# Ternary weights decided on VectorE beside an attention stage, in another order, and a token mixer's row-maximum scores one place ahead

## The reference

```python
# layer 0: token mixer (q, k, v are 32 rows each), attention, feed-forward with ternary weights
h = tok(x)                                   # softmax(q'k / sqrt(32)) v over 512 tokens, 128 sequences
h = h + attn0(layernorm(h))                  # 32 query heads, 8 key heads, head size 16, rope
h = h + ffn0(layernorm(h), w1, w3, w2)
# layer 1: attention, then a feed-forward with 4-bit weights
def ternary_quant(w):                        # of w1, w3 (1365 x 512) and w2 (512 x 1365)
    s = jnp.mean(jnp.abs(w))
    return jnp.clip(jnp.round(w / s), -1.0, 1.0) * s
```

## Time and profile before

| | us |
|---|---|
| median of 3 runs | 2435.5 |
| lowest and highest of the 3 | 2434.01, 2435.65 |
| the profiled execution's own time | 2430.69 |
| its span in the profile | 2428.5 |
| mean granted TensorE clock of it | 0.978 |
| PE busy in the span | 2243.3 (92%) |
| DVE busy | 1666.4 (69%) |
| ACT busy | 1495.8 (62%) |
| POOL busy | 1008.6 (42%) |

### The profile page before, as it was taken

The page is one execution under the profiler, slowest core; times in us unless marked ns, Lnnn a source line. Parts: engine busy times, 40 slices in busy tenths (PEclk is TensorE's granted clock), DMA queues, the critical chain, the costliest instruction groups (busy, mean ns, idle before and its releaser), DMA issues. The chain is left out here.

```text
span 2428.5 us, 41174 instructions
## 1 busy us (share of the span) xinstructions
PE 2243.3 (92%) x13188; PEld 1128.8 (46%) x13188; DVE 1666.4 (69%) x2937; ACT 1495.8 (62%) x2398; POOL 1008.6 (42%) x1002
## 2 busy tenths in 40 slices
PE   7999999998999994999999994999986999999998
PEld 2333333335666662444444443666652344444443
DVE  6666666656889886555556734666647888888874
ACT  4666666667787793445455514676645666667673
POOL 1222222238777771022223402444434555555552
PEclk9999999999999997999999997999998999999999
DMA  5544544532343211122222212222211111111101
GB/s 147 138 126 131 136 129 127 149 88 66 117 139 94 66 54 49 48 76 76 73 77 88 66 57 91 81 85 82 78 53 41 31 44 49 40 53 44 44 27 52
DMA packets 144444, 195.00 MB, mean 80 GB/s; under 512 B 32789, under 2 KB 76405, under 8 KB 144298
## 3 DMA queue, kind: packets, MB, share of 16 engines
q1 hardware_dynamic: 116890, 157.48, 21.5%
q10 hardware_dynamic: 27408, 35.66, 5.3%
HBM read 125.17 MB, written 42.21 MB: 69 GB/s over the span
## 5 line engine op out<-in xcount | busy, mean ns | idle before, releaser
L339 DVE TENSOR_REDUCE tm_negmax<-tm_s 128x1 f32<-128x512 f32 x512 | 323.3, 679 | 164.3 <-PE tm_s L382 164.0
L301 ACT ACTIVATE tm_prob<-tm_s 128x1024 f32<-128x1024 f32 x256 | 257.6, 1023 | 136.5 <-PE tm_s L402 130.7
L2271 PE MATMUL f_part<-f_xhi,gu 128*128 128x512 f16 x704 | 269.1, 382 | 18.3 <-ACT f_firstg L2090 6.6
L2271 PE MATMUL f_part<-f_xlo,gu 128*128 128x512 f16 x704 | 268.3, 381 | 0.0
L419 PE MATMUL tm_o<-tm_prob,tm_vt 128*64 128x512 f32 x1024 | 255.7, 620 | 0.0
L2059 POOL TENSOR_TENSOR f_firstg<-f_firstg,f_secondg 128x512 f32<-128x512 f32 x88 | 150.6, 1711 | 190.6 <-DVE f_secondg L2167 190.6
L2293 PE MATMUL f_pz<-dn,f_ghi 128*128 128x512 f16 x704 | 214.1, 379 | 5.8 <-ACT f_zc L2122 5.8
L382 PE MATMUL tm_s<-tm_qk 96*128 96x512 f16 x512 | 199.1, 391 | 14.8 <-DMA tm_qk<-tm_xs 14.3
L262 POOL TENSOR_TENSOR tm_hn<-tm_nd,tm_rows 128x1024 f32<-128x1024 f32 x32 | 75.3, 2353 | 292.9 <-DMA tm_rows<-rden 292.9
L402 PE MATMUL tm_s<-tm_qk 98*128 98x512 f16 x512 | 194.0, 382 | 1.3 <-DMA tm_qk<-tm_mrow 1.3
L969 PE MATMUL a_bankB<-a_wo,a_yThi 128*128 128x512 f16 x512 | 156.3, 388 | 4.1 <-DVE a_yTlo L892 4.0
(11 more groups left out here) (193 smaller groups left out, 5658.6 us busy)
## 6 DMA issues: line engine op xcount, KB each, us to landing
tm_qk<-tm_xs SPq DMA_DIRECT2D x384, 64.0 KB, 2.1
tm_xqk<-in_qk ACTq DMA_DIRECT2D x32, 512.0 KB, 4.4
a_hin<-h SPq DMA_DIRECT2D x64, 256.0 KB, 2.7
a_hres<-h SPq DMA_DIRECT2D x64, 256.0 KB, 3.0
h<-a_hout SPq DMA_DIRECT2D x64, 256.0 KB, 2.5
f_hin<-h SPq DMA_DIRECT2D x64, 256.0 KB, 2.8
f_hres<-h SPq DMA_DIRECT2D x64, 256.0 KB, 2.8
tm_vt<-in_vt ACTq DMA_DIRECT2D x32, 256.0 KB, 3.0
```

What stands on the lines that cost most here:

```text
L301: nc.scalar.activation(prob[b][:, 2 * h:2 * h + 2, :], s2[:, i % 2, :, :], ACT.Exp, scale=SCALE).then_inc(exp_done, 1)
L339: nc.vector.tensor_reduce(negmax[u][:, m:m + 1], s1[:, p % BANKS, :], AX.X, ALU.max, negate=True).then_inc(s1_read, 1)
L2271: last = nc.tensor.matmul(part[q % BANKS][:, :], (gate, up)[which][:, j, m * P:(m + 1) * P], xparts[x][u][:, j, :], start=x == 0, stop=x == 1)
```

## The change

It does five things.

1. `LEAD` becomes 15: the maximum scores run one place further ahead, and the numbers of the bank uses shift with it.
2. The down matrix is loaded first (n = 5 to 8) and the gate and up blocks after it (n = 9 to 16). VectorE sums the down blocks at n = 7 to 12, ScalarE the others at n = 11 to 18.
3. There are two totals: one of the down matrix at n = 14 and one of gate and up at n = 20, each with its own wait of TensorE for VectorE.
4. VectorE decides the down blocks one by one at the ends of steps 15 to 20, not after steps 32 and 33.
5. ScalarE's Sign and Relu are gone. VectorE decides a gate or up block with an is_lt (now L1329) and the `scalar_tensor_tensor` (now L1331), at the ends of steps 22 to 29.

```diff
-    LEAD = 14
+    LEAD = 15
@@ place, turned, use, freed @@
-        return 0 if m == 0 else m + 1 if m < 9 else m + 2
+        return m if m < 2 else m + 1 if m < 10 else m + 2
-        return 1 if pair else 10
+        return 2 if pair else 11
-            return p - (p > 1)
+            return p - (p > 2)
-            return 0 if t == 0 and p - BANKS == 1 else use(t, p - BANKS) + 1
+            return 0 if t == 0 and p - BANKS == 2 else use(t, p - BANKS) + 1
@@ ternary_weights @@
-    def totals(pe, tiles):
-        pe.wait_ge(summed, 8)
+    def totals_down(pe, tiles):
         pe.wait_ge(summed2, last // 2 + 1)
         pe.wait_ge(att.q_copied, tiles)
-        nc.tensor.matmul(total, ones[:, :], rows[:, :, :].rearrange("p i c -> p (i c)"), start=True, stop=False)
+        nc.tensor.matmul(total[:, 10:15], ones[:, :], rows[:, 2, :], start=True, stop=False)
         nc.tensor.matmul(total[:, 14:15], ones[0:rest, :], last_rows[0:rest, :], start=False, stop=True)\
             .then_inc(totalled, 1)
         pe.wait_ge(added, 1)
+    def totals_gates(pe, tiles):
+        pe.wait_ge(summed, 8)
+        pe.wait_ge(att.q_copied, tiles)
+        nc.tensor.matmul(total[:, 0:10], ones[:, :], rows[:, 0:2, :].rearrange("p i c -> p (i c)"), start=True, stop=True)\
+            .then_inc(totalled, 1)
+        pe.wait_ge(added, 2)
-    def below_block(act, i, j):
-        nc.scalar.activation(signs, stage[i][:, j * M:(j + 1) * M], ACT.Sign, bias=bounds[:, 0, i:i + 1])\
-            .then_inc(signed, 1)
-        nc.scalar.activation(below[n % 2], signs, ACT.Relu, scale=-1.0).then_inc(below_done, 1)
     def decide_block(dve, i, j):
         n = 4 * i + j
+        c = slice(j * M, (j + 1) * M)
         dve.wait_ge(bounded, 9)
+        if n >= 2:
+            dve.wait_ge(decided, n - 1)
+        nc.vector.tensor_scalar(below[n % 2], stage[i][:, c], bounds[:, 1, i:i + 1], None, ALU.is_lt).then_inc(below_done, 1)
         dve.wait_ge(below_done, n + 1)
         nc.vector.scalar_tensor_tensor(flat(targets[i])[:, c], stage[i][:, c], bounds[:, 0, i:i + 1], below[n % 2],
                                        ALU.is_gt, ALU.subtract).then_inc(decided, 1)
     def beside_scalar(act, n):
-        if 7 <= n <= 14:
-            sum_block(act, *divmod(n - 7, 4))
-        if 24 <= n <= 31:
-            below_block(act, *divmod(n - 24, 4))
+        if 11 <= n <= 18:
+            sum_block(act, *divmod(n - 11, 4))
     def beside_vector(dve, n):
-        if 15 <= n <= 20:
-            sum_blocks(dve, n - 15)
-        if n == 22:
-            set_bounds(dve)
-        if 25 <= n <= 32:
-            decide_block(dve, *divmod(n - 25, 4))
-        if n >= 32:
-            for c in range(3 * (n - 32), 3 * (n - 31)):
-                decide_blocks(dve, c)
+        if 7 <= n <= 12:
+            sum_blocks(dve, n - 7)
+        if n == 14:
+            set_bounds(dve, 2, 3, 1)
+        if 15 <= n <= 20:
+            decide_blocks(dve, n - 15)
+        if n == 20:
+            set_bounds(dve, 0, 2, 2)
+        if 22 <= n <= 29:
+            decide_block(dve, *divmod(n - 22, 4))
     def beside_tensor(pe, n):
-        if n == 22:
-            totals(pe, n + 2)
-            totals_read(pe)
+        if n == 14:
+            totals_down(pe, n + 2)
+        if n == 20:
+            totals_gates(pe, n + 2)
-TERNARY_LOADS = {5: [(0, 0)], 6: [(0, 1)], 7: [(0, 2)], 8: [(0, 3)], 9: [(1, 0)], 10: [(1, 1)], 11: [(1, 2)], 12: [(1, 3)],
-                 13: [(2, 0), (2, 1), (2, 2)], 14: [(2, 3), (2, 4), (2, 5)], 15: [(2, 6), (2, 7), (2, 8)], 16: [(2, 9), (2, 10)]}
+TERNARY_LOADS = {5: [(2, 0), (2, 1), (2, 2)], 6: [(2, 3), (2, 4), (2, 5)], 7: [(2, 6), (2, 7), (2, 8)], 8: [(2, 9), (2, 10)],
+                 9: [(0, 0)], 10: [(0, 1)], 11: [(0, 2)], 12: [(0, 3)], 13: [(1, 0)], 14: [(1, 1)], 15: [(1, 2)], 16: [(1, 3)]}
```

More of the change, by code:

```diff
@@ L1264, in ternary_weights @@
     flat = lambda t: t[:, :, :].rearrange("p j n -> p (j n)")
-    cleared, summed, summed2, totalled, added, bounded, signed, below_done, decided, below2_done, decided2 = (
-        sem("tw_" + n) for n in "cleared summed summed2 totalled added bounded signed below_done decided below2_done "
+    cleared, summed, summed2, totalled, added, bounded, below_done, decided, below2_done, decided2 = (
+        sem("tw_" + n) for n in "cleared summed summed2 totalled added bounded below_done decided below2_done "
         "decided2".split())
@@ L1292, in sum_blocks, with set_bounds @@
                                     apply_absolute_value=True).then_inc(summed2, 1)
-    def totals(pe, tiles):
-        pe.wait_ge(summed, 8)
+    def totals_down(pe, tiles):
         pe.wait_ge(summed2, last // 2 + 1)
         pe.wait_ge(att.q_copied, tiles)
-        nc.tensor.matmul(total, ones[:, :], rows[:, :, :].rearrange("p i c -> p (i c)"), start=True, stop=False)
+        nc.tensor.matmul(total[:, 10:15], ones[:, :], rows[:, 2, :], start=True, stop=False)
         nc.tensor.matmul(total[:, 14:15], ones[0:rest, :], last_rows[0:rest, :], start=False, stop=True)\
             .then_inc(totalled, 1)
-    def totals_read(pe):
         pe.wait_ge(added, 1)
-    def set_bounds(dve):
-        dve.wait_ge(totalled, 1)
-        nc.vector.tensor_reduce(sums[:, :], total.rearrange("p (i c) -> p i c", i=3), AX.X, ALU.add).then_inc(added, 1)
-        dve.wait_ge(added, 1)
-        for i in range(3):
+    def totals_gates(pe, tiles):
[4 more added lines that the diff above has]
+        pe.wait_ge(added, 2)
+    def set_bounds(dve, first, end, turn):
+        dve.wait_ge(totalled, turn)
+        nc.vector.tensor_reduce(sums[:, first:end], total[:, 5 * first:5 * end].rearrange("p (i c) -> p i c", c=5),
+                                AX.X, ALU.add).then_inc(added, 1)
+        dve.wait_ge(added, turn)
+        for i in range(first, end):
             for sign, to in ((0.5, bounds[:, 0, i:i + 1]), (-0.5, bounds[:, 1, i:i + 1]), (1.0, scales[:, i:i + 1])):
@@ L1313, in set_bounds @@
                     .then_inc(bounded, 1)
-    def below_block(act, i, j):
-        n = 4 * i + j
-        act.wait_ge(bounded, 9)
-        act.wait_ge(summed, 8)
-        if n:
-            act.wait_ge(below_done, n)
-        nc.scalar.activation(signs, stage[i][:, j * M:(j + 1) * M], ACT.Sign, bias=bounds[:, 0, i:i + 1])\
-            .then_inc(signed, 1)
-        act.wait_ge(signed, n + 1)
-        if n >= 2:
-            act.wait_ge(decided, n - 1)
-        nc.scalar.activation(below[n % 2], signs, ACT.Relu, scale=-1.0).then_inc(below_done, 1)
     def decide_block(dve, i, j):
         n = 4 * i + j
+        c = slice(j * M, (j + 1) * M)
         dve.wait_ge(bounded, 9)
+        if n >= 2:
+            dve.wait_ge(decided, n - 1)
+        nc.vector.tensor_scalar(below[n % 2], stage[i][:, c], bounds[:, 1, i:i + 1], None, ALU.is_lt).then_inc(below_done, 1)
         dve.wait_ge(below_done, n + 1)
-        c = slice(j * M, (j + 1) * M)
         nc.vector.scalar_tensor_tensor(flat(targets[i])[:, c], stage[i][:, c], bounds[:, 0, i:i + 1], below[n % 2],
@@ L1342, in decide_blocks @@
         to = below2[r, 0:cols.stop - cols.start]
-        dve.wait_ge(bounded, 9)
+        dve.wait_ge(bounded, 3)
         if c:
```

## The result

The changed kernel takes 2441.03 us in the median of 20 runs (2436.02 to 2443.37); the kernel before, on the same chip in the same session, 2433.96 (2429.84 to 2438.36). The ratio is 1.0027, with a 95% interval of 1.0021 to 1.0033: slower by 7.07 us, where +6.8 was forecast (2442.3 against a median of 2435.5 in the three earlier runs). The profiled execution of the changed kernel took 2440.29 (span 2438.1), 9.6 more than that of before (2430.69).

A forecast was written before the change was run, and what follows sets the result against it. In attention 0 a closed loop of waits through VectorE was taken to bound the steps. Terms 20.3 - 7.0 - 6.5 gave +6.8 us: 2437.5 from the profiled execution, 2442.3 in the runs' terms; range 2428 to 2452, likeliest case 2436 to 2448.

The forecast's parts named there:

- five down blocks, places 15 to 20: Attention 0, n = 15 to 19: X of 3.56 makes each step 13.01, 1.43 over 11.58; five cost 7.15 us.
- sixth block and second total, 20 to 22: Attention 0: half-size sixth down block with six short bound operations, the second total falling where TensorE waits anyway; 0.7 us.
- gate and up blocks, less the old total and the old ScalarE bound, 22 to 31: Attention 0: seven gate or up steps 14.2 and step 29 1.2, less old total 0.78 and ScalarE-bound steps 4.27.
- a_turn's share: Attention 0: VectorE's a_turn work meets GpSimd's products later; 0.1 us in each of 13 steps, 1.3 in all.
- end of attention 0: Last a_hout no longer behind three down pairs; next block's first VectorE instruction at 949.45 in place of 956.43: -7.0 us.
- mixer: Turn stops waiting, its follower waits instead; gain 0.11 us over 62 turns, 6.8, less 0.3 at the start: -6.5.
- 9.45 + X: Attention 0: shortest step through VectorE's loop of waits; X runs from ternary work's start to next a_hout; 11.58 for sums.
- The gate block's X: Attention 0, n = 22 to 28: is_lt, decision and GpSimd waits up to a_hout take 4.16 us; a step 13.61.
- behind the cast by 0.14: Attention 0, ends of steps: the decision on VectorE ends 0.14 us behind GpSimd's cast, counted in each block's X.
- the rival of 8 x 0.60 more: Gate and up blocks: the odd 1365-element is_lt is slow, 8 x 0.60 us more, 2447.1; chance 0.12.
- GpSimd does not get in between: Attention 0: is_lt, decision and a_kp run without GpSimd between; gate X 3.21, down 2.61; 2428.8, faster; chance 0.2.
- TensorE's clock falls: Gate steps: 3 us at the lower clock level in each of eight, 1.5 us of work each; +12, 2454; chance 0.07.

The follow-up runs named there:

- e3: Changed kernel with the gate and up blocks' VectorE is_lt replaced by a ScalarE Sign one step ahead, VectorE taking the smaller: 2426.99 us, ratio 0.9975 to the kernel before.
- e9: Changed kernel with GpSimd's four value instructions (cast, a_vhi, a_vrest, a_vlo) at one head of eight for places 23 to 30: 2437.27 us, ratio 1.0009.
- e6: Changed kernel with GpSimd's cast and a_vhi at one head of eight for places 23 to 30: 2437.16 us, ratio 1.0014 to the kernel before.
- e4: Changed kernel with a second, unread is_lt right ahead of the first in each of the eight gate and up blocks: 2453.04 us, ratio 1.0083.
- e7: Changed kernel with the gate and up blocks' is_lt moved ahead of a_pTlo, the decision staying at the step's end: 2432.31 us, ratio 0.9999.
- e1: Kernel before with only the mixer's part of the change (LEAD 15, the turn after the first maximum scores): 2426.82 us, ratio 0.9974.

## Why the prediction was right, point by point

| term | predicted | measured, from the a_mx starts of the two traces |
|---|---|---|
| sums moved, places 1 to 13 | 0 | 138.96 and 138.96: 0.00 |
| first total, places 13 to 15 | 0.8 | 24.06 - 23.16 = 0.90 |
| five down blocks, places 15 to 20 | 7.15 | 66.21 - 58.93 = 7.28 |
| sixth block and second total, 20 to 22 | 0.7 | 23.77 - 22.15 = 1.62 |
| gate and up blocks, less the old total and the old ScalarE bound, 22 to 31 | 10.35 | 120.11 - 109.07 = 11.04 |
| a_turn's share | 1.3 | none seen |
| end of attention 0 | -7.0 | -7.08 |
| mixer | -6.5 | -6.84 |
| sum | +6.8 | +6.92, and 7.07 in the medians |

**The loop** (9.45 + X) held. Down steps take 13.01, predicted 13.01; gate steps 13.54, predicted 13.61; from the measured X the formula gives 12.91 and 13.44, so the constant is nearer to 9.55. The exact hit on the down step is thus luck: its X was 0.10 too large (3.56 for 3.46) and the constant 0.10 too small. With 9.55, and X read from each trace at a gate step at full clock, the formula gives the steps of four other kernels within 0.01: e3 with X = 2.27 takes 11.82; e9 with 847.54 - 844.31 = 3.23 takes 12.77; e6 with 849.36 - 845.92 = 3.44 takes 12.98; e4 with 849.51 - 844.60 = 4.91 takes 14.45. That the loop sets the step is what these four and e7 show. The Trainium skill (SBUF — State Buffer, "Who interferes with whom") says that VectorE and GpSimd hold their shared port by turns for whole instructions; the stretched a_vhi, and a_kp's fall from 1.26 to 0.64 and 0.43 in e6 and e9, agree with it.

**The gate block's X** was 0.17 too large. The step of the text that was off is "behind the cast by 0.14": the cast had been issued during the is_lt and ended 0.14 behind it (847.53), and the decision, 1.64 long for the 1.77 of the sum, was not held. The other terms were right: 1.22 for 1.20, and a_vhi's end 0.90 behind the decision's for 0.95.

**The a_turn term** was not there. In its place stands one that I didn't see: the first step of each run of longer steps is longer still, 13.88 and 14.55, by 0.87 and 1.01, since a_mx moves against TensorE's rhythm when the loop closes, and only part returns when it opens. The rows of before have it (12.47 and then 10.57 around the sum blocks, cut at places 15 and 20), and with sums it cancels. (In the changed kernel the window of 13.88 holds 140 matmuls, the next ones 106.) It fits the 1.62 of places 20 to 22 and the 11.04 against 10.35; no run was made for it. The two errors nearly cancel (20.84 against 20.3), so the sum looks better than its parts.

**The mixer**: a wait of 0.18 behind the turn was predicted and is there. Whether 0.3 was lost at the start no run shows: the whole gain was 6.84 in one profile and 6.4 in e1, with the same code up to there, 6.2 in e1's median, and its steady part, behind the fourth turn, 6.1 to 6.3, about 0.10 a turn. The 6.84 in the sum has 0.69 from a start that varies by more than that, so part of the closeness of 6.92 to 7.07 is luck.

**The odd is_lt** kept the faster rate: 1.22 with its wait, against 1.10 on average for the 1024-element one. The Trainium skill (VectorE: DVE Perf Modes, "What auto-detection actually checks") allows that for rows of equal length on both sides; this trace agrees, and the rival of 8 x 0.60 more falls.

**The other rivals.** "GpSimd does not get in between" falls by the rows of step 18 and by e6 and e9, in which most of its price appears once GpSimd has little to do (12.77; it had said 12.66 for a gate step). "TensorE's clock falls" was false at 1.8 us of idle time in a step and true at 2.7 (e4), at a price close to the forecast's: 3.5 us at the lower level and 1.7 us more work, for 3 and 1.5, but only in every second step.

**What had no term** is the transition's granted clock. It put 2.5 us into the profiles' difference, 9.6 where the medians have 7.1. How often each length of it comes in the timed runs isn't known.

## What to carry to other kernels

Price an added instruction by the loop of waits in which it stands, not by the idle share of its engine: time the loop once with a block that is just hidden, and every further 0.1 us is then paid; here the port shared with GpSimd added GpSimd's next instruction at the border that the change made. Before an instruction is moved to the engine that closes the loop, look for a form that needs one instruction there: the smaller of (w > s/2) and sign(w + s/2) does a ternary decision with one on each of two engines, and with the early down weights it turned +7 into -12 to -15 us. Compare profiles stage by stage, and set aside a stage that differs between executions of one program before explaining it by the edit.
